# Two attention stages of a fused transformer kernel: fp32 products split in three rounded passes, PSUM banks shared out anew, work placed anew

## Chip, cores and metric

One core of one Trainium2 chip. The metric is the device time of one execution of the whole program in microseconds (median of several runs).

## Reference

The program computes two transformer layers on x of 4 x 2048 tokens of width 512. Each layer is cross attention (16 heads of width 32, 154 keys for each batch) on the layer-normed tokens, with a residual, then a feed-forward part: 32 experts with the top 8 of each token in layer 0, a light and a routed heavy branch in layer 1. The change touches the attention of both layers:

```python
q = split_heads(layernorm(x) @ Wq.T + bq)
k, v = split_heads(ctx @ Wk.T + bk), split_heads(ctx @ Wv.T + bv)
p = softmax((q @ k.T * tau + delta) / sqrt(32))
x = x + merge_heads(p @ v) @ Wo.T + bo
```

All is float32.

## The kernel before

`build` runs phases one after another: keys and values, `token_phase` of layer 0 (attention, and the logits of the gate), choice of the expert slots, the experts, `token_phase` of layer 1, the mixed phase (light branch) and the heavy phase. The change is in `token_phase` alone.

`token_phase` works on 16 groups of 512 tokens. Each engine runs one program of **turns** (i from -1 to 17), and a turn has 16 **units** (`st` or `u`): 4 heads (head group g = u // 4) of 128 tokens (t = u % 4). The order on each engine is written out by hand, by unit numbers; semaphores tie the engines together. In turn i, unit u:

- PE: `scores(i, u)`, four matmuls of 154 columns into two PSUM banks, 2*(u%2) and the next (so units alternate between banks 0, 1 and 2, 3); it waits for the exponentials of unit u-2. Then some of: `values` (P times V, five matmuls, lines 764 and 767), `x_turn` and `z_turn` (transposes, line 710), the gate's products. Then `streamed(st)`: half of one 512-column block of a dense product, which is k-chunks (0, 1) in an even unit and (2, 3) in an odd one. These are `query` (line 785, x @ Wq, for this group or the next) or `project` (line 806, O @ Wo, of the group before). Last `p_transposes` of unit u-2 (lines 734 and 735).
- DVE: `p_out` of unit u-3 (line 494: transposed P out of PSUM), `maximum` (line 471: the row maxima of the scores), `inverse` of unit u-1 (line 486), then what is placed there: layer-norm statistics (448), `normed` (460), `query_high` (69), `residual` (503), half of the transposed x out of PSUM (508), logits (521 to 532), in layer 1 `dot` (538).
- ACT: the four exponentials of a unit (line 691, each followed by a read of its accumulator), `query_out` (612), `o_out` (619: attention output out of PSUM), `p_tail_out` (624), the other half of the transposed x (629).
- POOL: `normalize` of unit u-1 (414: P times 1/sum), `query_low` (407), bias onto the residual (439), the powers of the norms (400).
- SP: all transfers in one queue. `stack_up(j, n)` (lines 339 to 349) lays head group n of q out as the stationary operand of the scores, 8 DMAs of the rounded part and 4 of the remainder; `load_kv`, the load of x, the load of x for the residual (`xbo`), and the stores of x and z.

The dense products take plain float32 operands. The profile shows each such matmul of 512 columns as two MATMUL records. In the experts and the heavy phase the same kind of product is already made by `product` (lines 72 to 76): each operand is split in a rounded part (`high`, type fp32r) and a remainder (`low`), and three passes are summed:

```python
pe.matmul(out, left[0], right[0], start=start, stop=False)
pe.matmul(out, left[0], right[1], start=False, stop=False)
return pe.matmul(out, left[1], right[0], start=False, stop=stop)
```

PSUM has 8 banks: 0 to 3 scores, 4 and 5 transposed P, 6 (`A_BANK`) dense products, 7 (`B_BANK`) the values' output and all other transposes, in turn.

Of the kernel before, what the change touches and what calls it, by code (L numbers as in the profile page):

```python
# [20 lines left out]
P = 128  # L21
# [9 lines left out]
TG = 4  # L31
# [213 lines left out]
def token_phase(nc, l, a, scr, c, x_in, x_rows):  # L245
    gate = l == 0
    with ExitStack() as ctx:
# [3 lines left out]
        wq, wo = sb("wq", [P, DC, D]), sb("wo", [P, DC, D])  # L251
# [4 lines left out]
        xn, xnT = sb("xn", [P, TG, D]), sb("xnT", [P, TG, D])  # L256
        oT = sb("oT", [P, 2, TG, D])
        qhigh, qlow = (sb(f"q_{part}", [P, 2, D], F32R) for part in ("high", "low"))
        qT = sb("qT", [P, 2, D])
        stack = sb("stack", [KROWS, HEADS, D], F32R)  # L260
# [13 lines left out]
        else:  # L274
# [5 lines left out]
                 "w_in wq_in kv_in0 kv_in1 kv_in2 kv_in3 x_in xbo_in ready ones x_stored z_stored "  # L280
                 "stacked0 stacked1 stacked2 stacked3 x_stats x_mv x_ve x_rstd xn xbo xnT_mm xnT_dve xnT_act "
                 "q_mm q_out q_high q_low scored negmax exped inv normed p_mm pTm pTt pv oT_out proj resid "
# [3 lines left out]
        W_IN = 16 * 4  # L286
        A_BANK, B_BANK = 6, 7
        STACK = 16 * 3 * HG
        Q_NEXT, Q_OWN = {10: 0, 14: 1}, {0: 2, 2: 3}
        O_AT, V_AT = {4: 0, 6: 1, 8: 2, 12: 3}, {7: 0, 11: 1}  # L290
        X_AT, Z_AT = {6: 0, 8: 1, 9: 2, 10: 3}, {2: 0, 4: 1, 5: 2, 12: 3}
# [18 lines left out]

        def load_kv(sp, j, g, used=0):
# [13 lines left out]
        def _(sp):  # L325
            sp.dma_start(x[:], rows(x_in, 0)).then_inc(s["x_in"], 16)
            sp.dma_start(wq[:], a[f"WqT{l}"].rearrange("(k p) n -> p k n", p=P)).then_inc(s["wq_in"], 16)
# [5 lines left out]
            sp.dma_start(wo[:], a[f"WoT{l}"].rearrange("(k p) n -> p k n", p=P)).then_inc(s["w_in"], 16)  # L333
# [5 lines left out]
            def stack_up(j, n):  # L339

                sp.wait_ge(s["q_high"], DC * j + n + 1)
                for at in (0, 2 * DK):
                    for h in range(HG):
                        sp.dma_start(stack[at:at + DK, HG * n + h, :].bitcast(F32),
                                     qhigh[h * DK:(h + 1) * DK, n % 2, :].bitcast(F32)).then_inc(s[f"stacked{n}"], 16)
                sp.wait_ge(s["q_low"], DC * j + n + 1)
                for h in range(HG):
                    sp.dma_start(stack[DK:2 * DK, HG * n + h, :].bitcast(F32),
                                 qlow[h * DK:(h + 1) * DK, n % 2, :].bitcast(F32)).then_inc(s[f"stacked{n}"], 16)

            def turn(i, par, prev2, prev, cur, nxt, nxt2):
                if cur:
                    stack_up(i, 1)
                if prev2 and gate:
                    sp.wait_ge(s["z"], TG * (i - 1))
                    sp.dma_start(rows(scr["xw"], i - 2, D), z[:]).then_inc(s["z_stored"], 16)
                if cur:
                    stack_up(i, 2)
                if prev and cur:
                    load_kv(sp, i, 2, GROUPS * i - 1)  # L360
                    load_kv(sp, i, 3, GROUPS * i)
                if nxt2:
                    reached(sp, s["xn"], TG * (i + 2))
                    sp.dma_start(x[:], rows(x_in, i + 2)).then_inc(s["x_in"], 16)
                if cur:
                    stack_up(i, 3)
                if cur and nxt:
                    load_kv(sp, i + 1, 0, GROUPS * i + 1)
                    load_kv(sp, i + 1, 1, GROUPS * i + 2)
                if nxt:  # L370
                    stack_up(i + 1, 0)
                if prev2 and not gate:
                    sp.wait_ge(s["z"], TG * (i - 1))
                    sp.wait_ge(s["score"], i - 1)
                    sp.dma_start(rows(scr["xs"], i - 2), z[:]).then_inc(s["z_stored"], 16)
                if prev:
                    sp.wait_ge(s["resid"], TG * i)
                    sp.dma_start(rows(x_rows, i - 1), xs[:]).then_inc(s["x_stored"], 16)
                if cur:
                    reached(sp, s["resid"], TG * i)  # L380
                    sp.dma_start(xbo[:], rows(x_in, i)).then_inc(s["xbo_in"], 16)

            turns(sp, turn)
# [4 lines left out]
        def _(pool):  # L388
# [14 lines left out]

            def query_low(j, n):
# [12 lines left out]
            def turn(i, par, prev2, prev, cur, nxt, nxt2):  # L417
                if isinstance(i, int) and i == 0:
                    pool.wait_ge(s["w_in"], W_IN)
                for st in range(UNITS):  # L420
                    if st == 3 and nxt:
                        rstd_of(0, "x", i + 1)
                    if st == 15 and prev:
                        rstd_of(1, "s", i - 1)
                    if st == 11 and prev2 and not gate:
                        pool.wait_ge(s["ssq_c"], i - 1)
                        pool.tensor_tensor(rn[:], ssq[:], half[:], ALU.pow).then_inc(s["rn"], 1)
                    if nxt and st == 12:
                        query_low(i + 1, 0)
                    if st >= 1 and cur:  # L430
                        normalize(i, st - 1)
                    if st == 0 and prev:
                        normalize(i - 1, UNITS - 1)
                    if cur and st in (0, 2, 4):
                        query_low(i, 1 + st // 2)
                    if st in (1, 5, 7, 9) and prev:
                        t = {1: 0, 5: 1, 7: 2, 9: 3}[st]
                        pool.wait_ge(s["xbo_in"], 16 * i)
                        pool.tensor_tensor(xbo[:, t, :], xbo[:, t, :], bo[:], ALU.add).then_inc(s["xbo"], 1)  # L439
# [4 lines left out]
        def _(dve):  # L444
# [23 lines left out]
            def maximum(i, u):  # L468
                dve.wait_ge(s["scored"], UNITS * i + u + 1)
                q = 2 * (u % 2)  # L470
                dve.tensor_reduce(negmax[:, u, :].rearrange("p (b h) -> p b h", b=2),  # L471
# [1693 lines left out]
```

## Time and profile before

| | |
|---|---|
| median of 3 runs | 3937.42 us (3932.35 to 3938.48) |
| the profiled execution | 3931.68 us, span 3930.0 us |
| mean granted TensorE clock | 0.947 of full speed |
| busy share: PE, DVE, POOL, ACT | 90%, 70%, 49%, 38% |
| token phase of layer 0 | about 120 to 1125 us |
| token phase of layer 1 | about 2202 to 3155 us |

A matmul's duration in the records is longer than its share of the engine, since matmuls overlap; what one costs is read from the starts of the records that follow one another. "x4" in a timeline is four records merged.

### The profile page before, as it was taken

Reading aid. Unit: us, or ns where it says so; the run is one execution under the profiler, and the core shown is the slowest. Engines: PE = TensorE matmul, PEld = TensorE weight load, DVE = VectorE, ACT = ScalarE, POOL = GpSimd, SP = SyncE. Lnnn points to the kernel's source line nnn. Section 1 sums busy time; section 2 is a strip of 40 time slices with the busy share of each in tenths; the row PEclk is TensorE's granted clock in tenths of the full one; section 3 lists DMA queues with packets and bytes.
Section 4 is the critical chain, followed back from the end, with each engine's and each line's share of the span. In section 5 each row is a group of like instructions: output and inputs, shape, how many; then the busy total and the mean of one; then the engine's idle time right before and its main releaser. Section 6 shows DMA issues by size and latency. Waiting matters only on the chain. (4 is left out here: it accounts for less than half of the span.)

```text
span 3930.0 us, 55737 instructions
## 1 busy us (share of the span) xinstructions
PE 3518.3 (90%) x16111; PEld 2376.0 (60%) x16111; DVE 2744.7 (70%) x5462; ACT 1506.5 (38%) x5254; POOL 1921.5 (49%) x1789
## 2 busy tenths in 40 slices
PE   8599999999946799999999599999999958879998
PEld 4355555555525677777777355555555536657776
DVE  3477777777669676776767367777777758766665
ACT  0256666666610111111111166666666634211110
POOL 0255555555510567677776355555565633223322
PEclk9799999999975899999999799999999979989999
DMA  5454555555420566666666444654654447521101
GB/s 162 134 146 139 144 161 141 144 156 146 119 76 11 156 162 163 161 165 169 155 173 149 109 133 134 172 146 133 169 153 141 131 147 273 188 97 22 18 12 14
DMA packets 323310, 523.14 MB, mean 133 GB/s; under 512 B 59352, under 2 KB 104216, under 8 KB 322648
## 3 DMA queue, kind: packets, MB, share of 16 engines
q1 hardware_dynamic: 290904, 443.79, 37.9%
q0 software_dynamic: 32256, 77.65, 10.4%
q8 instruction: 58, 0.95, 0.1%
q14 instruction: 92, 0.75, 0.1%
HBM read 283.64 MB, written 136.96 MB: 107 GB/s over the span
## 5 line engine op out<-in xcount | busy, mean ns | idle before, releaser
L691 ACT ACTIVATE t_pr<-ps,t_negmax 128x154 f32<-128x154 f32 x2048 | 867.8, 547 | 530.8 <-DVE t_negmax L471 530.4
L414 POOL TENSOR_TENSOR t_pr<-t_pr,t_inv 128x616 f32<-128x616 f32 x512 | 639.8, 1251 | 620.7 <-DVE t_inv L486 618.1
L494 DVE COPY t_pTm<-ps 128x512 f32<-128x512 f32 x512 | 350.0, 684 | 316.7 <-PE ps L735 312.6
L785 PE MATMUL ps<-t_xnT,t_wq 128*128 128x512 f32 x1024 | 506.2, 618 | 19.4 <-ACT t_qT L612 19.1
L806 PE MATMUL ps<-t_wo,t_oT 128*128 128x512 f32 x1024 | 501.1, 613 | 7.6 <-DVE t_xs L503 6.5
L734 PEld LDWEIGHTS ps<-ident,t_pr 128*128 128x128 f32 x2048 | 318.2, 204 | 295.6 <-issue 262.5
L691 ACT ACTIVATION_READ_ACCUMULATOR t_pr<-ps,t_negmax 128x1 f32 x2048 | 471.8, 230 | 0.0
L471 DVE TENSOR_REDUCE t_negmax<-ps 128x4 f32<-128x616 f32 x512 | 403.1, 787 | 28.5 <-PE ps L722 28.0
L734 PE MATMUL ps<-ident,t_pr 128*128 128x128 f32 x2048 | 334.2, 286 | 51.2 <-DVE t_pTm L494 37.6
L722 PE MATMUL ps<-t_kst,t_stack 98*128 98x154 f32 x2048 | 340.0, 289 | 13.4 <-DMA t_stack<-t_q_low 13.0
L785 PEld LDWEIGHTS ps<-t_xnT,t_wq 128*128 128x128 f32 x1024 | 176.9, 192 | 230.1 <-issue 203.4
L74 PE MATMUL ps<-e_xT_high,e_wgu_high 128*128 128x512 f32 x768 | 307.2, 400 | 1.6 <-DVE e_xT_low L1248 1.6
L76 PE MATMUL ps<-e_xT_high,e_wgu_low 128*128 128x512 f32 x768 | 304.7, 397 | 0.0
L75 PE MATMUL ps<-e_xT_low,e_wgu_high 128*128 128x512 f32 x768 | 302.7, 394 | 0.0
L806 PEld LDWEIGHTS ps<-t_wo,t_oT 128*128 128x128 f32 x1024 | 176.9, 192 | 186.8 <-issue 167.5
L722 PEld LDWEIGHTS ps<-t_kst,t_stack 98*128 98x128 f32 x2048 | 272.7, 194 | 19.2 <-issue 18.0
L1208 POOL DMA_INDIRECT x_dram<-e_y,e_put_idx x128 | 246.1, 1923 | 30.8 <-issue 30.5
L1316 ACT ACTIVATE e_sig<-ps 128x512 f32<-128x512 f32 x96 | 57.5, 599 | 527.4 <-PE ps L76 387.8
L407 POOL TENSOR_TENSOR t_q_low<-t_qT,t_q_high 128x512 fp32r<-128x512 f32 x128 | 176.3, 1377 | 167.5 <-DVE t_q_high L69 167.5
L1288 DVE TENSOR_TENSOR e_h<-e_sig,ps 128x512 f32<-128x512 f32 x96 | 65.8, 685 | 245.0 <-issue 200.4
L1937 POOL TENSOR_TENSOR h_w_low<-c_hw,h_w_high 128x512 fp32r<-128x512 f32 x64 | 89.6, 1403 | 249.0 <-DVE h_w_high L69 249.0
L439 POOL TENSOR_TENSOR t_xbo<-t_xbo,t_bo 128x512 f32<-128x512 f32 x128 | 166.2, 1300 | 62.4 <-DMA t_xbo<-x_dram 61.8
(297 smaller groups left out, 7297.0 us busy)
## 6 DMA issues: line engine op xcount, KB each, us to landing
t_stack<-t_q_high SPq DMA_DIRECT2D x1024, 64.0 KB, 2.1
e_wgu_in<-in_gate_upT SPq DMA_DIRECT2D x32, 1536.0 KB, 6.6
t_stack<-t_q_low SPq DMA_DIRECT2D x512, 64.0 KB, 2.0
x_dram<-t_xs SPq DMA_DIRECT2D x32, 1024.0 KB, 5.6
t_kst<-kst_dram SPq DMA_DIRECT2D x128, 235.8 KB
e_wd_in<-in_downT SPq DMA_DIRECT2D x32, 768.0 KB
xs_dram<-t_z SPq DMA_DIRECT2D x16, 1032.0 KB
l_z<-xs_dram SPq DMA_DIRECT2D x16, 1032.0 KB
```

The source lines that it names most:

```text
L74: pe.matmul(out, left[0], right[0], start=start, stop=False)
L75: pe.matmul(out, left[0], right[1], start=False, stop=False)
L76: return pe.matmul(out, left[1], right[0], start=False, stop=stop)
L414: pool.tensor_tensor(p, p, inv[:, v, :].unsqueeze(1).to_broadcast([P, KEYS, HG]), ALU.mult).then_inc(s["normed"], 1)
L471: dve.tensor_reduce(negmax[:, u, :].rearrange("p (b h) -> p b h", b=2), ps[:, q:q + 2, 0:2 * KEYS].rearrange("p b (h n) -> p b h n", h=2), ...
L494: dve.tensor_copy(pTm[:, g % 2, :, t * P:(t + 1) * P], ps[:, 4, :].rearrange("p (h n) -> p h n", h=HG)).then_inc(s["pTm"], 1)
L691: op = act.activation(pr[:, u % 4, :, h], ps[:, 2 * (u % 2) + h // 2, at:at + KEYS], ACT.Exp, bias=negmax[:, u, h:h + 1], accum_out=total[ ...
L722: mm = pe.matmul(ps[:, 2 * (u % 2) + h // 2, at:at + KEYS], stack[:, HG * g + h, t * P:(t + 1) * P], kst[:, g, h * KEYS:(h + 1) * KEYS], s ...
L734: pe.transpose(ps[:, 4, h * P:(h + 1) * P], pr[:, v % 4, 0:P, h], ident[:])
L785: mm = pe.matmul(ps[:, A_BANK, :], wq[:, k, n * P:(n + 1) * P], xnT[:, k, :], start=(k == 0), stop=(k == DC - 1))
L806: mm = pe.matmul(ps[:, A_BANK, :], oT[:, par, k, t * P:(t + 1) * P], wo[:, k, :], start=(k == 0), stop=(k == DC - 1))
L1208: pool.indirect_dma_start(out=scr["x1"][:, :], out_offset=bass.IndirectOffsetOnAxis(ap=put_idx[:, n:n + 1], axis=0), in_=y[q][:, n, :], in ...
```

## The change

In both token phases:

- **Split products.** Wq and Wo lie in SBUF as `high` and `low` (fp32r). They are loaded into `xs` and `z` (free at the start) and split there: `weight_high` on ACT, `weight_low` on POOL, four chunks each. The transposed x is rounded out of PSUM by ACT (`x_turned`, all four chunks) and its remainder is made by DVE (`x_low`, four); attention output likewise (`o_out` on ACT, `o_low` on DVE, new, four in a turn). `query` and `project` call `product`: three passes for one float32 matmul. The copies of x's halves on DVE (line 508) go.
- **Scores on three banks.** Heads lie 170 columns apart in one flat range: a unit has three heads in a bank of its own and one in bank 1, which both units share. The matmul into bank 1 comes last and waits (`shared`) for the first exponential of the unit before, which reads that unit's head in bank 1.
- **Bank 3 for transposes** of x, z and the gate; `values` keeps bank 7.
- **x is normed in place** (`xn` goes), so the next load of x waits for the transposes; `stack` holds two head groups in place of four; `oT` holds six chunks.
- **New placement.** Jobs are placed by half unit (`at`, 0 to 31; what belongs to a unit on DVE, ACT and POOL runs at the odd half), in a table for each layer; the SP order is written out for each layer.

```diff
-        wq, wo = sb("wq", [P, DC, D]), sb("wo", [P, DC, D])
+        wq = [sb(f"wq_{part}", [P, DC, D], F32R) for part in ("high", "low")]
+        wo = [sb(f"wo_{part}", [P, DC, D], F32R) for part in ("high", "low")]
-        stack = sb("stack", [KROWS, HEADS, D], F32R)
+        stack = sb("stack", [KROWS, 2 * HG, D], F32R)
...
+        T_BANK, A_BANK, B_BANK = 3, 6, 7
+        APART, BASE, SHARED = 170, (2, 854), (3, 0)
         Q_NEXT, Q_OWN = {10: 0, 14: 1}, {0: 2, 2: 3}
+        O_AT = {4: 0, 6: 1, 8: 2, 12: 3}
+        V = (14, 23, 2, 7) if gate else (15, 23, 3, 7)
+        X = (12, 15, 18, 20) if gate else (12, 16, 18, 20)
+        Z = (3, 8, 10, 25)
+        OL = (19, 30, 4, 9) if gate else (18, 29, 6, 10)
+        RES = (12, 15, 20, 28) if gate else (12, 15, 20, 27)
+        XL = (14, 18, 19, 22) if gate else (15, 18, 19, 21)
+        QH = (23, 1, 8, 15) if gate else (23, 2, 7, 15)
+        LOG = 31
+        SX = (1, 2, 3, 5) if gate else (0, 1, 1, 3)
+        NX = (8, 8, 8, 8) if gate else (6, 7, 8, 8)
+        SS = (14, 23, 25, 29) if gate else (16, 20, 26, 31)
+        NZ = (0, 0, 1, 2) if gate else (3, 6, 6, 11)
+        QO = (22, 0, 1, 5) if gate else (21, 0, 2, 5)
+        QL = (25, 1, 9, 16) if gate else (26, 3, 9, 19)
+        XB = (7, 10, 11, 20) if gate else (0, 4, 14, 18)
...
             def second_layer(i, par, prev2, prev, cur, nxt, nxt2):
...
+                if cur and nxt:
+                    load_kv(sp, i + 1, 0, GROUPS * i + 1)
+                    load_kv(sp, i + 1, 1, GROUPS * i + 2)
+                if nxt2:
+                    load_x(i + 2)
+                if nxt:
+                    stack_up(i + 1, 0)
...
+            def x_low(j, k):
+                dve.wait_ge(s["xnT_high"], DC * j + k + 1)
+                dve.tensor_tensor(xnT[1][:, k, :], ps[:, T_BANK, :], xnT[0][:, k, :].bitcast(F32),
+                                  ALU.subtract).then_inc(s["xnT_low"], 1)
...
                 reached(pe, s["exped"], UNITS * i + u - 1)
-                for h in range(HG):
-                    at = (h % 2) * KEYS
-                    mm = pe.matmul(ps[:, 2 * (u % 2) + h // 2, at:at + KEYS], stack[:, HG * g + h, t * P:(t + 1) * P],
+                for n in range(HG):
+                    h = (n + 1 + SHARED[u % 2]) % HG
+                    at = BASE[u % 2] + h * APART
+                    if n == HG - 1:
+                        reached(pe, s["shared"], UNITS * i + u)
+                    mm = pe.matmul(flat[:, at:at + KEYS], stack[:, HG * (g % 2) + h, t * P:(t + 1) * P],
                                    kst[:, g, h * KEYS:(h + 1) * KEYS], start=True, stop=True)
...
-                    mm = pe.matmul(ps[:, A_BANK, :], wq[:, k, n * P:(n + 1) * P], xnT[:, k, :],
-                                   start=(k == 0), stop=(k == DC - 1))
+                    mm = product(pe, ps[:, A_BANK, :], [w[:, k, n * P:(n + 1) * P] for w in wq],
+                                 [v[:, k, :] for v in xnT], k == 0, k == DC - 1)
```

`V`, `X`, `Z` are the half units at which PE runs `values`, `x_turn` and `z_turn`; `OL`, `XL`, `RES`, `QH`, `SX`/`SS`, `NX`/`NZ` and `LOG` those at which DVE runs `o_low`, `x_low`, `residual`, `query_high`, the statistics, `normed` of x and z, and the logits; `QO` is `query_out` on ACT, `QL` and `XB` are `query_low` and the bias on POOL.

## Rows read from the trace of the kernel before

**Rows 1.** Busy time by window (PE, PEld, DVE, ACT, POOL): a stretch of each layer

```profile
2500.00:2620.00 120.00, 115.30 (x549) 67.28 (x548) 91.96 (x198) 81.10 (x321) 71.14 (x61) 0.99 0.53 147
...
500.00:620.00 120.00, 118.19 (x594) 70.42 (x593) 90.02 (x190) 72.36 (x292) 66.24 (x58) 1.00 0.52 150
```

**Rows 2.** Timeline of PE (start, us, op): same place of two turns, each layer

```profile
508.84 1.98 PE L785 MATMUL ps<-t_xnT,t_wq 128*128 128x512 f32 x4
...
510.66 0.63 PE L734 MATMUL ps<-ident,t_pr 128*128 128x128 f32 x4
...
568.16 1.98 PE L785 MATMUL ps<-t_xnT,t_wq 128*128 128x512 f32 x4
...
2507.29 1.99 PE L785 MATMUL ps<-t_xnT,t_wq 128*128 128x512 f32 x4
...
2564.38 1.98 PE L785 MATMUL ps<-t_xnT,t_wq 128*128 128x512 f32 x4
```

**Rows 3.** Group of lines of DVE, experts (busy, mean ns, idle before)

```profile
L1248 DVE TENSOR_TENSOR e_xT_low<-ps,e_xT_high 128x512 fp32r<-128x512 f32 x128 | 88.5, 691 | 4.4
```

**Rows 4.** Timeline of PE, one unit of layer 0

```profile
549.18 0.65 PE L722 MATMUL ps<-t_kst,t_stack 98*128 98x154 f32 x4
...
549.66 0.61 PE L710 MATMUL ps<-ident,t_z 128*128 128x128 f32 x4
...
550.11 1.88 PE L806 MATMUL ps<-t_wo,t_oT 128*128 128x512 f32 x4
...
551.83 0.63 PE L734 MATMUL ps<-ident,t_pr 128*128 128x128 f32 x4
...
552.33 0.65 PE L722 MATMUL ps<-t_kst,t_stack 98*128 98x154 f32 x4
```

**Rows 5.** Timeline of PE, expert phase, two matmuls six apart

```profile
1402.23 0.48 PE L74 MATMUL ps<-e_xT_high,e_wgu_high 128*128 128x512 f32 x1
...
1403.72 0.39 PE L74 MATMUL ps<-e_xT_high,e_wgu_high 128*128 128x512 f32 x1
```

**Rows 6.** PE groups, idle before: layer 0 500.5:619.2, then layer 1 2500:2620

```profile
L785 PE MATMUL ps<-t_xnT,t_wq 128*128 128x512 f32 x65 | 31.8, 610 | 1.2 <-ACT t_qT L612 1.2
...
L734 PE MATMUL ps<-ident,t_pr 128*128 128x128 f32 x128 | 20.4, 282 | 0.4 <-DVE t_pTm L494 0.2
...
L734 PE MATMUL ps<-ident,t_pr 128*128 128x128 f32 x132 | 21.2, 284 | 3.1 <-DVE t_pTm L494 3.1
```

**Rows 7.** Timelines of DVE and ACT, the same unit of layer 0

```profile
549.46 0.69 DVE L494 COPY t_pTm<-ps 128x512 f32<-128x512 f32 x1 [3.23 <-PE ps L735]
...
550.07 0.79 DVE L471 TENSOR_REDUCE t_negmax<-ps 128x4 f32<-128x616 f32 x1
...
550.89 0.54 ACT L691 ACTIVATE t_pr<-ps,t_negmax 128x154 f32<-128x154 f32 x1
```

**Rows 8.** Timelines of DVE, POOL and PE, layer 0; its start-up; its gate logits

```profile
521.41 3.77 DVE L460 TENSOR_SCALAR t_xn<-t_x,t_mv,t_rstd 128x512 f32<-128x512 f32 x4
...
522.53 1.46 POOL L407 TENSOR_TENSOR t_q_low<-t_qT,t_q_high 128x512 fp32r<-128x512 f32 x1
...
525.93 0.72 PE L734 MATMUL ps<-ident,t_pr 128*128 128x128 f32 x4 [0.22 <-DVE t_pTm L494]
...
133.33 1.91 DVE L460 TENSOR_SCALAR t_xn<-t_x,t_mv,t_rstd 128x512 f32<-128x512 f32 x4 [1.52 <-POOL t_rstd L400]
...
561.06 0.66 DVE L521 TENSOR_REDUCE t_logit<-ps 128x128 f32<-128x512 f32 x1
...
562.52 0.68 DVE L494 COPY t_pTm<-ps 128x512 f32<-128x512 f32 x1
```

**Rows 9.** Timelines of SP and PE, layer 1, the end of a turn

```profile
2568.80 4.96 SPq L344 DMA_DIRECT2D t_stack<-t_q_high  x8
...
2573.80 2.49 SPq L348 DMA_DIRECT2D t_stack<-t_q_low  x4
...
2577.98 0.65 PE L722 MATMUL ps<-t_kst,t_stack 98*128 98x154 f32 x4
```

More of the change, by code:

```diff
@@ L352, in turn @@
                 if cur:
                     stack_up(i, 1)
-                if prev2 and gate:
-                    sp.wait_ge(s["z"], TG * (i - 1))
-                    sp.dma_start(rows(scr["xw"], i - 2, D), z[:]).then_inc(s["z_stored"], 16)
+                    stack_up(i, 2)
+                if prev and cur:
+                    load_kv(sp, i, 2, GROUPS * i - 1)
+                if cur:
+                    stack_up(i, 3)
+                if prev2:
+                    store_z(i - 2, i - 1)
@@ L357, in turn, with second_layer @@
+            def second_layer(i, par, prev2, prev, cur, nxt, nxt2):
+                if cur:
+                    stack_up(i, 1)
+                if prev and cur:
+                    load_kv(sp, i, 2, GROUPS * i - 1)
                 if cur:
@@ L369, in turn @@
                     load_kv(sp, i + 1, 1, GROUPS * i + 2)
+                if nxt2:
+                    load_x(i + 2)
                 if nxt:
                     stack_up(i + 1, 0)
[L372 to L375, printed above, removed]
+                if prev2:
+                    store_z(i - 2, i - 1)
+                if cur:
+                    load_xbo(i)
                 if prev:
[L377 to L383, printed above, removed]
+                    store_x(i - 1)
+            turns(sp, first_layer if gate else second_layer)
             sp.wait_ge(s["z_stored"], 16 * NG)
@@ L417, in turn @@
             def turn(i, par, prev2, prev, cur, nxt, nxt2):
+                if isinstance(i, int) and i == -1:
+                    for k in range(DC):
+                        pool.wait_ge(s["wq_high"], k + 1)
+                        weight_low(wq, xs, k, "wq_low")
                 if isinstance(i, int) and i == 0:
@@ L430, in turn @@
[L430 to L439, printed above, removed]
+                    if isinstance(i, int) and i == 0 and 6 <= st < 6 + DC:
+                        pool.wait_ge(s["wo_high"], DC)
+                        weight_low(wo, z, st - 6, "wo_low")
@@ L579, in turn @@
-                    if prev and st in (6, 8, 10, 14):
-                        t = min(st - 6, 6) // 2
+                        for t in range(TG):
+                            if at == SX[t]:
+                                statistics(0, "x", i + 1, x, (t,))
+                        for t in range(TG):
+                            if at == NX[t]:
+                                normed(0, "x", i + 1, x, x, "xn", (t,))
+                    if at in SS and prev:
+                        t = SS.index(at)
@@ L805, in project, with x_turn @@
                 for k in chunks:
[L806 to L807 removed]
+                    mm = product(pe, ps[:, A_BANK, :], [v[:, o_slot(par, k), t * P:(t + 1) * P] for v in oT],
+                                 [w[:, k, :] for w in wo], k == 0, k == DC - 1)
                 if DC - 1 in chunks:
                     mm.then_inc(s["proj"], 1)
[L811 removed]
+            def x_turn(j, k, prev2):
```

406 lines of the change are left out of this document (218 added, 188 removed).

## Prediction

> **What bounds the kernel now.** I read the busy time by window first. In a stretch of 120 us of the token phases PE is busy for 118.2 us in layer 0 and 115.3 us in layer 1, DVE for 90.0 and 92.0, POOL for 66 and 71 [rows 1]. So PE sets the pace of both phases, and DVE is next with a quarter of its time free. Then the timeline of PE: the same matmul comes back after 568.16 - 508.84 = 59.32 us in layer 0 and after 57.09 us in layer 1 [rows 2]; that is one turn, and there are 16 in each layer. PE's own waits are about 0.95 us a turn in layer 0 (its groups' idle times in two turns sum to 1.9; the largest is 1.2 for `query_out`) and about 2.3 us in layer 1 (4.8 in 2.1 turns; 3.1 of it in the transposes of P, for DVE's copy) [rows 6].
>
> **The products.** A chunk of a dense product (two float32 matmuls, four records) takes 551.83 - 550.11 = 1.72 us behind transposes [rows 4], and 510.66 - 508.84 = 1.82 us behind other matmuls [rows 2]. The three-pass form of the same size runs in the experts: six passes behind transposes take 1403.72 - 1402.23 = 1.49 us [rows 5]. So a chunk gets shorter by 0.23 to 0.33 us; I take 0.29, nearer the second, since most chunks stand behind scores or values. A layer has 16 x 16 chunks, two layers 512: **-148 us** (bounds -118 and -169).
> The Trainium skill (TensorE: Matmul & The Clock Gate, "Back-to-back issue gap") gives N/2.4 + 2.5 ns for one pass, 216 ns here; six would be 1.30 us and the saving at 0.42 to 0.52 us a chunk some 240 us, an estimate from that page. The row shows 1.49 us with the weight loads in it, and the sum goes by the row.
>
> **The work that is added.** DVE loses two copies a turn and gains four `x_low` and four `o_low`: an instruction of that kind takes 691 ns [rows 3], and one such step 0.61 us from start to start (550.07 - 549.46) [rows 7], so some +4 us a turn. DVE had 90.0/120 x 59.32 = 44.5 us in a turn [rows 1, 2]; it will have 48.6 of the 54 to 55 that PE then takes in layer 0, and about 48 (92.0/120 x 57.09 = 43.8, and 4) of 52 in layer 1. ACT gains two copies on 36 us of busy time a turn, POOL nothing in a steady turn: both stay hidden behind PE. DVE no longer is: at 90% what counts is when each job comes.
>
> **How late DVE may be.** In a plain unit PE will take 0.48 (scores, 549.66 - 549.18) + 1.46 (a chunk, between 1.40 and 1.49) + 0.50 (transposes of P, 552.33 - 551.83) = 2.45 us [rows 4]. DVE's fixed part is `p_out` 0.61, `maximum` 0.70, `inverse` 0.09: 1.40 us. The new wait `shared` ties the last score matmul of unit u+1 to the maximum and first exponential of unit u. Counted from the scores' start at 549.18: maximum over and ACT at it at +1.71 [rows 7], the first exponential with its read over at about +2.3; PE gets there at 2.45 + 0.37 = +2.8. So **DVE may be late by 0.5 us** and what PE has between (transposes 0.44, values 1.98). Before, PE waited for the unit before that, and only `p_out` bound it: a norm of four tiles that held DVE for 3.7 us cost PE 0.22 us [rows 8].
>
> **Layer 0, unit by unit** (DVE's jobs by the placement against PE's time; 0.6 us for a statistics, residual or low job, 0.4 for `query_high`). Into unit 0 come the logits, 1.46 us [rows 8], and two norms of z. One tile of `normed` takes 1.91/4 = 0.48 us where POOL is idle and 3.77/4 = 0.94 where POOL works beside it [rows 8]. The norms behind the logits come when POOL's `normalize` is over, so they cost 0.48 each: 1.4 + 1.46 + 1.0 = 3.9 us against PE's 2.9. The 1.0 us of lateness goes into 0.5 of slack and into PE's wait for `query_out`, which was 0.6 and stays. Unit 1: two statistics, two norms, `query_high`, 4.7 us against 2.45, late by 2.8; PE has values and transposes there (2.4 + 0.5), so no stall, with nothing to spare. Unit 2 wins it back. Unit 4: four norms (3.7) and `query_high`, 5.5 us against 4.4, after 1.0 us of lateness from unit 3, with a slack of 0.94: a stall of 1.1. The rest fits. Sum 1.7 us; with the norms at 0.94 throughout it is 3.5. I take **2.4 us a turn** where it was 0.95.
> The Trainium skill (SBUF — State Buffer, "Who interferes with whom") has it that a copy or scalar operation of VectorE in a two-port mode and an instruction of GpSimd exclude each other, and that the one issued second waits for the whole of the first. The trace agrees, with 3.77 us against 1.91 for the same four norms; if it holds at each place, the stall of a turn is nearer 1.7 than 3.5 us.
>
> **Layer 1.** Unit 4 (three of the norms of x) is late by 1.3 to 1.9 us with a slack of 0.5: 0.8 to 1.4. And the stack: `stack_up` of group 0 for the next turn took SP 4.96 + 2.49 us, its last DMA was issued at about 2575.7 and PE began the next turn's scores at 2577.98, just behind its landing: no slack [rows 9]. Now its place is behind `load_kv`, which waits for the values at half unit 23, now behind the chunk, and behind the load of x. From unit 11's scores: values over 3.9, `load_kv` 1.65, `load_x` 0.6, stack 7.5, landing of the last 1.4: +15.1; PE is there after 4.4 + 4 x 2.45 = 14.2. So 0.9 us for it, which takes the place of the wait for `query_out`. **2.4 us a turn** where it was 2.3.
>
> **Once a layer.** Four `weight_low` on POOL (1.4 us each, as [rows 8]) stand before the first `rstd`, 5.5 us, of which half is hidden by the loads and by the shorter fill of `stack`; each first transpose of x now waits for ACT and DVE in turn. 3 to 8 us, taken as 5: **+10 us** in all.
>
> **Sum.** -148 + 16 x (2.4 - 0.95) + 16 x (2.4 - 2.3) + 10 = -148 + 23 + 2 + 10 = -113 us on the profiled 3931.7: 3819. The median of the runs shown lies 5.7 us above that execution, so the time forecast is **3824 us**, 2.9% less. The layer-0 turn would be 59.3 - 4.6 + 1.4 = 56.1 us, the layer-1 turn 57.1 - 4.6 + 0.1 = 52.6 us.
>
> **Rivals.**
> *A: the placement is exact and PE waits for almost nothing.* For it: every large DVE job stands where PE has values or transposes beside it, and ACT's waits for a query stand likewise. Against it: my sums for unit 4 in both layers. All waits but 0.6 us a turn go: -148 - 52 + 19 + 10 = -171, 3766 us.
> *B: DVE is the bound, at 90% in order.* Norms and copies run into POOL, each late unit stalls PE by `shared` instead of being won back. Layer 0 at 4.5 us of waits, layer 1 at 4.5: -148 + 57 + 35 + 10 = -46, 3891 us. For it: a slack of 0.5 us where it was over 1.5. Against it: the free units 5 to 9 and 12 to 15.
> *C, slower than before: the queue of SP becomes the pace.* With two groups in `stack` a group can be laid out only when the group two before is scored, and each takes 7.5 us of SP's issue, on top of `query_low` on POOL and the landing, with `load_kv` and whole loads of x between. My sums leave 2 to 4 us in every group but the one above. It decides where each group is late by 1.5 us: 6 us a turn more in 32 turns is +192 on 3824 less the 29 counted, 3987; the point of no gain is 3.5 us a turn beyond my sum. Against it: SP is issuing for some 39 of 55 us (four groups of 7.5, twelve loads of keys and values at 0.55, four large transfers at 0.6).
> *D: the change does not do what it says*, and the passes here cost no less than float32. The scores are of that type already and the experts run it; what could eat the gain is the added wait inside each unit: nothing, or at most half of a score matmul (0.48/4/2 = 0.06 us) x 512 = 30 us. That is in the range.
>
> **Numbers.** About 0.2% (8 us) is what a measurement of this kernel can tell from no change. Chances: the forecast (3790 to 3860) 0.50, A 0.20, B 0.20, C 0.08, D 0.02. Faster by over 0.2%: 0.88; within: 0.03; slower: 0.09. The range that should hold 8 in 10 reaches from A to B: 3765 to 3890 us.
>
> **What would show it.** In the changed profile the starts of product passes should lie 0.23 to 0.25 us apart, in sixes of 1.40 to 1.49 us. The turns should be 56 and 52.6 us. DVE's share in a turn should be 87 to 92%. The score group of line 722's successor should show idle time ended by ACT's exponential (`shared`) at units 1 to 5, and in layer 1 a wait for a stack DMA at the start of a turn. Idle time of over 4 us a turn on PE would prove me wrong towards B, with SP's rows ending it towards C; under 1 us, towards A.

## The result and the profile after

The changed kernel takes 3956.7 us (median of 4 runs, 3950.9 to 3961.4) where the kernel before takes 3934.9 (4 runs beside them): ratio 1.0057, 95% interval 1.004 to 1.0073. The forecast was 3824 us and 88% for faster. It is slower by 0.6%, with an interval that leaves out 1, and the time lies 67 us above the range of 3765 to 3890.

The page of the changed kernel, its first two parts:

```profile
span 3949.2 us, 58011 instructions
...
PE 3417.9 (87%) x17135; PEld 2612.1 (66%) x17135; DVE 2848.8 (72%) x5654; ACT 1543.9 (39%) x5334; POOL 1930.6 (49%) x1805
...
PEclk9799999999975799999999799999999979989999
```

The same two stretches as in [rows 1], busy time by window (PE, PEld, DVE, ACT, POOL, then the granted clock, the DMA share and GB/s):

```profile
500.00:620.00 120.00, 108.52 (x633) 81.75 (x631) 90.53 (x191) 70.40 (x284) 63.00 (x56) 0.94 0.51 142
2500.00:2620.00 120.00, 108.60 (x626) 82.50 (x625) 102.26 (x210) 84.19 (x328) 70.16 (x61) 0.97 0.53 151
```

PE was busy for 118.2 and 115.3 us of the 120; now it is for 108.5 and 108.6, and its granted clock is 0.94 and 0.97 where it was 1.00 and 0.99. So PE stands still for some 11 us in each stretch. The waits of the two token phases tell for what (us in total, times, longest), first layer 0 (320 to 1100 us), then layer 1 (2350 to 3140 us):

```profile
PE ps L847 <- DVE t_pTm L583: 33.6, 17, 5.9
DVE t_z L549 <- issue: 33.1, 5, 6.7
...
PE ps L835 <- DMA t_vt<-vt_dram: 26.4, 13, 4.4
...
PE ps L74 <- ACT t_qT L713: 6.6, 13, 0.5
```

```profile
POOL t_xbo L528 <- DMA t_xbo<-x_dram: 96.8, 14, 7.9
...
PE ps L847 <- POOL t_pr L494: 50.1, 14, 4.6
...
PE ps L74 <- ACT t_qT L713: 8.1, 13, 1.0
PE ps L835 <- ACT t_pr L778: 6.9, 13, 0.5
```

Three waits stand out, and none of them has a term in the forecast's sum.

**Stall 1, every second turn of layer 0.** The turns of layer 0 (from a `values` matmul to the same one a turn later) take 56 and 66 us in alternation. The loop over turns holds two of them, and the long one is where it jumps back. DVE and PE there:

```profile
503.71 0.17 DVE L627 COPY c_top<-t_top 128x32 f32 x1
510.49 1.00 DVE L549 TENSOR_SCALAR t_z<-t_xs,t_mv,t_rstd 128x512 f32<-128x512 f32 x2 [6.60 <-issue]
```

```profile
512.14 1.13 PE L847 MATMUL ps<-ident,t_pr 128*128 128x128 f32 x4 [5.83 <-DVE t_pTm L583]
...
514.05 2.00 PE L857 MATMUL ps<-t_pTt,t_vt 104*128 104x512 f32 x2
...
552.22 1.02 PE L857 MATMUL ps<-t_pTt,t_vt 104*128 104x512 f32 x2
```

The last instruction of the body ends at 503.88, the first of the next pass starts at 510.49, and the profile finds no semaphore for it ("issue"). PE stands still for 5.83 us and then works at half speed: the same `values` matmuls take 2.00 us at 514 and 1.02 at 552. The window after the stall shows a granted clock of 0.50 for 6 us, the level of 1.2 GHz (the kernel before has 1.00, the level of 2.4 GHz, at the same place of its turn, 510 to 516 us):

```profile
512.00:518.00 6.00, 5.86 (x20) 2.68 (x20) 5.92 (x12) 1.72 (x9) 3.29 (x3) 0.50 0.27 66
```

So the long turn is 10 us longer for 6.6 us on DVE. At the same jump the kernel before lost 0.33 us (its timeline of DVE):

```profile
503.11 0.17 DVE L532 COPY c_top<-t_top 128x32 f32 x1
503.61 0.69 DVE L494 COPY t_pTm<-ps 128x512 f32<-128x512 f32 x1 [0.33 <-issue]
```

Two things stand beside the stall of the changed kernel. SP had just issued three transfers of 1 MB (store of x, load of x, load for the residual); and among the packets of 502 to 512 us there are four of the kind "instruction", of which the kernel before has none there:

```profile
497.49 0.43 SPq L402 DMA_DIRECT2D x_dram<-t_xs  x1
498.19 0.41 SPq L398 DMA_DIRECT2D t_x<-in_x  x1
498.79 1.17 SPq L406 DMA_DIRECT2D t_xbo<-in_x  x1
```

```profile
q14 instruction: 4, 0.03, 1.0%
```

**Stall 2, every turn of layer 0.** PE at unit 12, and SP's queue just before:

```profile
554.75 0.27 PE L848 MATMUL ps<-ident,t_pr 128*104 128x128 f32 x1
557.28 0.68 PE L835 MATMUL ps<-t_kst,t_stack 98*128 98x154 f32 x4 [2.25 <-DMA t_vt<-vt_dram]
```

```profile
550.26 0.43 SPq L391 DMA_DIRECT2D xw_dram<-t_z  x1
550.88 0.34 SPq L359 DMA_DIRECT2D t_kst<-kst_dram  x1
551.41 0.76 SPq L359 DMA_DIRECT2D t_vm<-vm_dram  x1
552.35 1.06 SPq L359 DMA_DIRECT2D t_vt<-vt_dram  x1
```

The keys and values of head group 3 are loaded behind the store of 1 MB of z, and PE reaches them 2.25 us before they have landed.

**Stall 3, every turn of layer 1.** POOL, PE and SP at the start of a turn:

```profile
2594.38 1.26 POOL L528 TENSOR_TENSOR t_xbo<-t_xbo,t_bo 128x512 f32<-128x512 f32 x1 [7.19 <-DMA t_xbo<-x_dram]
2595.60 2.38 POOL L494 TENSOR_TENSOR t_pr<-t_pr,t_inv 128x616 f32<-128x616 f32 x2
```

```profile
2596.87 0.91 PE L847 MATMUL ps<-ident,t_pr 128*128 128x128 f32 x4 [3.82 <-POOL t_pr L494]
```

```profile
2585.08 0.44 SPq L394 DMA_DIRECT2D xs_dram<-t_z  x1
2585.72 0.39 SPq L406 DMA_DIRECT2D t_xbo<-x_dram  x1
```

The first bias of layer 1 stands at half unit 0 (`XB = (0, ...)`). Its load is issued at 2585.72, behind another store of 1 MB, and lands at about 2594. POOL stands in that wait for 7.19 us, and `normalize` of two units stands behind it on POOL (the "x2" at 2595.60): PE waits 3.82 us for P.

What was forecast of the passes is there too. Six passes of a chunk (layer 0, at another place of the same turn) take 552.22 - 550.78 = 1.44 us; behind the first, their starts lie 0.23 us apart (four of the six shown):

```profile
550.78 0.44 PE L74 MATMUL ps<-t_xnT_high,t_wq_high 128*128 128x512 f32 x1
551.06 0.39 PE L75 MATMUL ps<-t_xnT_low,t_wq_high 128*128 128x512 f32 x1
551.29 0.39 PE L76 MATMUL ps<-t_xnT_high,t_wq_low 128*128 128x512 f32 x1
551.52 0.39 PE L74 MATMUL ps<-t_xnT_high,t_wq_high 128*128 128x512 f32 x1
```

### The profile page after: what moved, and what is told of

Its sections match the earlier page's. It is cut to its first block and busy times, and to the rows that moved or that the text cites. A ratio compares the mean times of both kernels' runs of the same rounds, so it can differ in the third digit from the quotient of the medians.

```text
span 3949.2 us, 58011 instructions
## 1 busy us (share of the span) xinstructions
PE 3417.9 (87%) x17135; PEld 2612.1 (66%) x17135; DVE 2848.8 (72%) x5654; ACT 1543.9 (39%) x5334; POOL 1930.6 (49%) x1805
## 5 line engine op out<-in xcount | busy, mean ns | idle before, releaser
L778 ACT ACTIVATION_READ_ACCUMULATOR t_pr<-ps,t_negmax 128x1 f32 x2048 | 484.7, 237 | 0.0
L847 PE MATMUL ps<-ident,t_pr 128*128 128x128 f32 x2048 | 357.7, 299 | 111.4 <-POOL t_pr L494 57.2
L835 PE MATMUL ps<-t_kst,t_stack 98*128 98x154 f32 x2048 | 365.3, 298 | 59.9 <-DMA t_vt<-vt_dram 28.0
L835 PEld LDWEIGHTS ps<-t_kst,t_stack 98*128 98x128 f32 x2048 | 291.3, 201 | 76.8 <-DMA t_vt<-vt_dram 31.5
L1400 ACT ACTIVATE e_sig<-ps 128x512 f32<-128x512 f32 x96 | 57.5, 599 | 527.2 <-PE ps L76 527.2
L74 PE MATMUL ps<-t_xnT_high,t_wq_high 128*128 128x512 f32 x512 | 228.1, 446 | 18.6 <-ACT t_qT L713 18.6
L74 PE MATMUL ps<-t_wo_high,t_oT_high 128*128 128x512 f32 x512 | 221.6, 433 | 4.7 <-DVE t_xs L592 4.7
L75 PE MATMUL ps<-t_xnT_low,t_wq_high 128*128 128x512 f32 x512 | 210.1, 410 | 0.0
L76 PE MATMUL ps<-t_xnT_high,t_wq_low 128*128 128x512 f32 x512 | 209.9, 410 | 0.0
L76 PE MATMUL ps<-t_wo_high,t_oT_low 128*128 128x512 f32 x512 | 206.3, 403 | 0.0
```

Of the source, the lines that this page charges most:

```text
L778: op = act.activation(pr[:, u % 4, :, h], flat[:, col:col + KEYS], ACT.Exp, bias=negmax[:, u, h:h + 1], accum_out=total[:, u, h:h + 1])
L835: mm = pe.matmul(flat[:, at:at + KEYS], stack[:, HG * (g % 2) + h, t * P:(t + 1) * P], kst[:, g, h * KEYS:(h + 1) * KEYS], start=True, sto ...
L847: pe.transpose(ps[:, 4, h * P:(h + 1) * P], pr[:, v % 4, 0:P, h], ident[:])
```

## Experiments

Each time stands against runs of the kernel before on the same chip (3931 to 3934 us).

### One repair at a time, and all three

```diff
# e1: VectorE's turns written out
-            turns(dve, turn)
+            unrolled(turn)
# e2: first_layer, layer 0
+                if prev and cur:
+                    load_kv(sp, i, 3, GROUPS * i)
                 if prev2:
                     store_z(i - 2, i - 1)
-                if prev and cur:
-                    load_kv(sp, i, 3, GROUPS * i)
# e3: the bias of layer 1 later
-        XB = (7, 10, 11, 20) if gate else (0, 4, 14, 18)
+        XB = (7, 10, 11, 20) if gate else (7, 10, 14, 18)
# e4: e1, e2 and e3
```

> The changed kernel with DVE's program of the token phases written out turn by turn (as ACT's is) in place of a hardware loop over two turns; the instructions of a turn and their order are the same. Theory J (in layer 0 DVE stands still for some 6.6 us at the top of every second turn because after the jump back its instructions have to be fetched, behind 3 MB of data transfers just issued): layer 0's turns stop alternating between 56 and 66 us, all are about 56, the idle time before the norm of z ended by nothing that the profile shows is gone, and the time falls by 45 to 60 us. Rival Z (DVE waits there for the store of the z before, or for the transposes of z): the stall stays, the time moves by less than 8 us.

> The changed kernel with, in layer 0's queue of SP, the load of keys and values of head group 3 issued before the store of z, not behind it. Theory K (the 2.0 us a turn for which PE waits at unit 12 for that load are due to the 1 MB store issued just before it): that wait is gone, the time falls by 20 to 30 us. Rival (the values' end releases the buffer too late, or PE then waits for DVE at the same place): the wait shrinks by less than 1 us or is given back, the time falls by less than 10 us.

> The changed kernel with the first two additions of the bias onto the residual on POOL, layer 1, at half units 7 and 10 in place of 0 and 4 (as in layer 0), so POOL no longer stands waiting for the load of the residual before it normalizes P. Theory X (that wait, 7 us a turn on POOL, makes PE wait 3.6 to 3.8 us a turn in its transposes of P): PE's wait for POOL there is gone, layer 1's turns fall from 57.3 to 53 to 54 us, the time by 45 to 60 us. Rival B (DVE, full to 88%, is the bound of the turn whoever waits): PE waits for DVE's copies or maxima at that place, layer 1's turns fall by less than 1.5 us, the time by less than 20 us.

> The three edits together. If the three waits are independent, as the theories have it, their gains add: some 115 to 140 us less than the changed kernel, near 3825 us, which is 2.5 to 3% faster than the kernel before and what the prediction had summed. If DVE is the bound behind them (rival B), it stays above 3890 us.

`e4` is all of these edits in one kernel. The turns are read from the `values` matmuls of the profiled executions.

| kernel | median, us | ratio to before, 95% | turns of layer 0 | turns of layer 1 |
|---|---|---|---|---|
| changed | 3956.7 | 1.0057 (1.004 to 1.0073) | 56 / 66 | 57.0 to 57.5 |
| e1 | 3912.2 | 0.9941 (0.9924 to 0.9957) | 55.8 to 58.7 | 57.3 to 58.4 |
| e2 | 3917.9 | 0.9964 (0.995 to 0.9978) | 55.0 / 62 to 64 | 57.2 to 57.6 |
| e3 | 3888.3 | 0.9876 (0.9858 to 0.9894) | 56 / 66 | 52.7 to 52.8 |
| e4 | 3815.4 | 0.9694 (0.9677 to 0.971) | 54.9 to 56.3 | 52.7 to 53.5 |

Each stall goes with its own repair, and the steady turns of the other layer stay what they were. Alone the repairs are worth 44, 39 and 68 us (expected were 45 to 60, 20 to 30 and 45 to 60), together 141, 3956.7 - 3815.4, which is 10 us less than the sum of the three. In layer 1, e3 takes the turn to 52.7 us, where 52.6 was forecast; in layer 0, e4 takes it to about 55.5, where 56.1 was forecast. The three stalls are the whole distance between the forecast (3824 us) and the result; what lies under that agreement is taken up further down.

### What makes stall 1: the transfers, the jump, or the place of the code

```diff
# e5: layer 0, in the looped turns; e9: the same for load_x too
-                sp.dma_start(xbo[:], rows(x_in, j)).then_inc(s["xbo_in"], 16)
+                if gate and not isinstance(j, int):
+                    sp.dma_start(xbo[:, :, 0:P], rows(x_in, j, P)).then_inc(s["xbo_in"], 16)
```

> The changed kernel, but the residual's load of layer 0 brings only a quarter of its columns in the looped turns, so three quarters of the residual of layer 0 are left out (later results are then not the reference's). It asks why DVE stands still for 6.6 us at the start of every second turn of layer 0. Theory 1 (its instructions are fetched after the jump of its loop, behind three transfers of 1 MB that SP issued just before): with 2.25 MB instead of 3 in front of it the stall gets shorter, to about 4 us or less, the turns of 66 us become 62 to 64, and the time falls by 15 to 30 us from 3957. Theory 2 (the jump costs what it costs, whatever is being moved): the stall stays at 6 to 7 us, the turns at 66 us, the time within 5 us of 3957.

> The changed kernel, but in the looped turns of layer 0 both loads of x (for the norm and for the residual) bring a quarter of their columns, so three quarters of both are left out there. Bringing a quarter of the residual's load alone changed nothing, although the queues were empty some 3 us earlier; in the changed kernel four instruction packets lie at the jump of VectorE's loop (505.4, 506.9, 508.0, 510.9 us, the jump at 503.8), in the kernel before none. Theory 1 (the jump makes VectorE fetch its code anew, and the two loads of 1 MB in front stretch each fetch): with 0.5 MB in front the stall of 6.6 us falls to 3 us or less, the turns of 66 us to 62 or less, the time by 20 to 35 us from 3957. Theory 2 (the fetches follow each other at their own latency): the stall stays at 6 to 7 us and the time within 5 us of 3957.

Both kernels leave out three quarters of the columns of the loads named, so their output is not the reference's.

e5: 3958.0 us, ratio to before 1.0065 (1.005 to 1.0081): nothing gained, DVE's five waits sum to 32.9 us where they were 33.1. That is theory 2. e9: 3951.0 us, ratio 1.0047 (1.003 to 1.0064); the five waits sum to 26.1 us, the long turns are 64 us, the four instruction packets are still there. This lies between the two expectations. The jump at 498 us:

```profile
497.84 0.17 DVE L633 COPY c_top<-t_top 128x32 f32 x1
502.69 1.00 DVE L555 TENSOR_SCALAR t_z<-t_xs,t_mv,t_rstd 128x512 f32<-128x512 f32 x2 [4.68 <-issue]
```

The DMA engines are all but idle from 499.3 us on, but 4.7 of the 6.6 us are left. So the transfers stretch the stall by up to 2 us, and do not make it.

```diff
# e7: the kernel before
-            turns(dve, turn)
+            unrolled(turn)
# e10: the changed kernel, ahead of the turns
+            if gate:
+                for _ in range(64):
+                    dve.wait_ge(s["x_in"], 16)
             turns(dve, turn)
# e11: the kernel before, in DVE's turn
+                    if gate and prev2 and st in (3, 6, 9, 12):
+                        dve.wait_ge(s["x_in"], 16)
```

> The kernel before, with VectorE's turns written out instead of looped, the same edit that gave the changed kernel 44 us. Theory 1 (the stall comes of the changed order of SP's queue, three large transfers in front of the jump): the kernel before lost 0.33 us there in a turn pair of layer 0, and 1.4 us in seven places of layer 1, so nothing or at most 10 us is gained, 3921 to 3935 us. Rival (unrolled code is better for VectorE whatever the queue does): 30 us or more are gained here too, 3900 us or less.

> The changed kernel with 64 waits that are long fulfilled ahead of VectorE's turns of layer 0: they move its loop by 64 instructions and do nothing else, for at most 2 us once. Theory 3 (whether the jump finds its target still held depends on where the loop's code lies): the four instruction packets at each jump and the stall of 6.6 us go in layer 0, 30 to 45 us are gained, 3912 to 3927. Rival (the place has no part in it, only the length of the body, 293 instructions where it was 286, or what SP moves at the time): the stall stays, 3952 to 3960.

> The kernel before with four waits that are long fulfilled in each of VectorE's turns of layer 0, so that its loop's body has 294 instructions, as the changed kernel's (293), where it has 286. Theory 4 (the body became too long to be held over the jump): stalls and instruction packets appear at each jump of layer 0, 3 to 7 us each, and the time rises by 15 to 40 us from 3934. Rival (the length has no part in it): no stall over 1 us at the jump, and the time within 5 us of 3934.

e7: 3933.5 us, ratio 1.0 (0.999 to 1.0009). Written-out turns are worth nothing by themselves; e1's gain is the stall.

e10: 3926.7 us, ratio 0.9984 (0.9972 to 0.9995), 30 us less than the changed kernel. It has the same body and the same transfers, and some waits more ahead of the loop. The same jump, and the instruction packets around it:

```profile
497.84 0.17 DVE L627 COPY c_top<-t_top 128x32 f32 x1
498.50 1.00 DVE L549 TENSOR_SCALAR t_z<-t_xs,t_mv,t_rstd 128x512 f32<-128x512 f32 x2 [0.48 <-issue]
```

```profile
q14 instruction: 1, 0.01, 0.2%
```

In layer 0 the stall is down to 0.48 us, with the three transfers in full in front of it. And a new one has come in layer 1, whose code was moved along with the rest; its sum is 17.5 us in five places:

```profile
2447.89 0.69 DVE L537 BATCH_NORM_STATS2 t_stat<-t_x 128x6 f32<-128x512 f32 x1 [3.69 <-issue]
```

e11: 3969.5 us, ratio 1.0091 (1.0074 to 1.0108), 36 us more than the kernel before, for waits that are long fulfilled and of which no other effect is seen. The jump of layer 0 there:

```profile
509.95 0.17 DVE L532 COPY c_top<-t_top 128x32 f32 x1
517.02 0.69 DVE L494 COPY t_pTm<-ps 128x512 f32<-128x512 f32 x1 [6.91 <-issue]
```

```profile
517.77 1.13 PE L736 MATMUL ps<-ident,t_pr 128*128 128x128 f32 x4 [4.92 <-DVE t_pTm L494]
```

Its turns are 59.2 and 67 us in alternation, as those of the changed kernel are 56 and 66. So stall 1 has nothing to do with products, banks or the placement on PE.

What the long jumps have in common can be read from the records. The trace has the loop's branch itself and the first register operation of the body behind it. The nine looped runs have 90 such jumps in the two token phases. In 50 of them 0.22 to 0.29 us pass between the two, with no instruction packet in that time; in 40 of them 3.5 to 6.8 us pass, with one to three packets of 8 KB in it. Over four passes of the loop of layer 0 (380 to 860 us) there are 11 instruction packets in the kernel before, 32 in the changed one, 12 in e10 and 31 in e11; in layer 1 (2450 to 2920 us) there are 12, 12, 33 and 15. So a pass with a long jump brings some five packets, 40 KB, that one with a short jump does not bring. That VectorE fetches its code anew, since the target is no longer held, fits all of this. It remains an inference, since the records do not say for which engine a packet was.

Length and place both matter. The waits of e11 stand only in turns that have a group two before them, and the first of these is in the loop: the recorded instructions ahead of the loop are those of the kernel before, and its body has 290 where it was 286 (294 had been expected). So e11 changes the length alone, and the stall comes. e10 changes the place alone, by 32 recorded instructions, and the stall goes in layer 0 and comes in layer 1. The length by itself does not decide either: the body in layer 1 of the changed kernel has 298 and no stall, that in layer 0 has 293, in the changed kernel with the stall and in e10 without it. By what rule length and place go together no run here tells.

### Is PE's work the bound?

```diff
# e6: one pass, both products; project alike
-                    mm = product(pe, ps[:, A_BANK, :], [w[:, k, n * P:(n + 1) * P] for w in wq],
-                                 [v[:, k, :] for v in xnT], k == 0, k == DC - 1)
+                    mm = pe.matmul(ps[:, A_BANK, :], wq[0][:, k, n * P:(n + 1) * P], xnT[0][:, k, :],
+                                   start=(k == 0), stop=(k == DC - 1))
```

> The changed kernel with one pass instead of three in the products of q and o, so the two passes with a remainder are left out and q and the attention output carry the rounding of one operand pair. It asks what would bound the token phases if PE had 4 of 6 passes less in each chunk, 0.93 us. If PE's own work set all of the time, 512 chunks would give up to 475 us. Theory 1 (DVE, at about 48 of 56 us a turn, takes over almost at once): turns of layer 1 stay above 50 us, those of layer 0 too, and the whole gain is under 150 us. Theory 2 (PE's work is the bound and the late loads only add to it): turns of 45 us or less and a gain of over 300 us.

The kernel leaves out the two passes with a remainder. 3892.8 us, ratio 0.9895 (0.988 to 0.991): 64 us less than the changed kernel, for 512 x 0.93 = 476 us of work on PE less at the full clock. Turns are 55 to 57 and 62 to 63 us in layer 0 and 55 to 57 in layer 1, as theory 1 had it. Two things take the rest back. PE now waits for DVE (61.7 us for the copy of P in layer 1, where the changed kernel has 4.8), for `stack` (18.3 us there, 3.0 in the changed kernel) and for keys and values (51.1 us in layer 0, 26.4 in the changed kernel). And PE's granted clock is lower: 0.86 in the stretch of layer 0 and 0.84 in that of layer 1, where the changed kernel has 0.94 and 0.97. In 120 us of layer 1 some 31 us of passes are left out (14.9 us a turn), and PE is busy for only 12.7 us less (95.9 against 108.6). So the run shows that taking work from PE gives little while the stalls stand. How much of that is DVE and how much the clock it does not separate, and theory 1's reason, that DVE takes over, is shown in part only.

### A version better than both, and the products undone in it

```diff
# e8: e4, and first_layer loads x ahead of the first stack of the next turn
+                if nxt2:
+                    load_x(i + 2)
                 if nxt:
                     stack_up(i + 1, 0)
                 if prev:
                     store_x(i - 1)
-                if nxt2:
-                    load_x(i + 2)
# e12: e8, each chunk a float32 matmul of the rounded parts; project alike
+                    mm = pe.matmul(ps[:, A_BANK, :], wq[0][:, k, n * P:(n + 1) * P].bitcast(F32),
+                                   xnT[0][:, k, :].bitcast(F32), start=(k == 0), stop=(k == DC - 1))
```

> The changed kernel with all three repairs (VectorE's turns written out, the third load of keys and values ahead of the store of z in layer 0, the bias of layer 1 at half units 7 and up), and in layer 0 the load of x also ahead of the first stack of the next turn, some 8 us earlier. With the three alone DVE still waited 27.1 us in 12 places for x, and PE's waits for the copy of P and for the norm of z behind it came to 15 and 14 us in 13 turns. Theory 1 (x comes late and makes the units 2 to 4 late): DVE's wait goes and 8 to 20 us are gained on 3815, so 3795 to 3807. Rival (DVE wins the lateness back, PE has its work): within 5 us of 3815.

> The kernel with the three repairs and the earlier load of x (3798.6 us), with one part of the change undone: each chunk of q and o is again a plain float32 matmul (four records of 128 rows' width in place of six passes), on the rounded operands alone, so what the remainders add is left out; VectorE and ScalarE make the remainders all the same. It measures the one large term of the prediction by itself, 0.29 us a chunk in 512 chunks, -148 us (bounds -118 and -169). Theory (PE's work sets the pace once the stalls are gone): the time rises by 118 to 169 us, 3917 to 3968, the turns of layer 0 from 54.0 to 58 to 59 us, those of layer 1 from 52.7 to 57 us. Rival (VectorE, at over 90% in layer 1, had become the bound, and the passes' gain is partly lost to it): the rise is under 100 us.

e8: 3798.6 us, ratio 0.9655 (0.964 to 0.967), 17 us less than e4, as theory 1 said. The turns of layer 0 are 54.0 us throughout, DVE's wait for x is gone. The two stretches of before and after in e8:

```profile
500.00:620.00 120.00, 118.05 (x723) 90.19 (x722) 102.54 (x218) 81.42 (x330) 74.17 (x64) 1.00 0.56 153
2500.00:2620.00 120.00, 114.35 (x674) 85.88 (x666) 111.59 (x227) 92.04 (x361) 79.57 (x67) 1.00 0.57 159
```

e12: 3890.7 us, ratio 0.989 (0.9873 to 0.9906). It leaves out what the remainders add. Without the passes 92 us come back (104 between the two profiled executions). That is below the 118 to 169 of the theory and on the side of the rival (under 100 us: the gain is partly lost to VectorE). Where they are was read from the starts of PE's matmuls: time from the first of a group to the start of the next other group, us a turn, mean of 8 turns from 400 us and 8 from 2400 us on. A wait ahead of a group is counted with the group before it.

```
                        before      e12 float32    e8 passes
layer 0   turn          59.3        57.7           54.0
          products      28.8        28.1           24.2
          scores         9.2         8.5            8.9
          P transposed   8.1         8.2            8.6
          x, z transp.   3.7         3.6            3.2
          values         8.0         7.9            7.9
layer 1   turn          58.0        55.2           52.8
          products      31.1        28.2           24.6
          scores         8.6         8.7            9.8
          P transposed   8.2         8.7            9.1
```

From e12 to e8 the products give 4.0 and 3.6 us a turn, 0.25 and 0.22 a chunk. The transposes of x and z give another 0.4 and 0.3, since the passes start sooner behind them. The scores (with them the wait `shared`, and in layer 1 the stack) take back 0.4 and 1.1, the transposes of P 0.4 in each. From before to e12, with the products as they were, 42 us are gained, some 17 of them by the earlier load of x that e12 has from e8. In the steady turns that is 1.6 us in layer 0 and 2.8 in layer 1; over all 16 turns of a layer (first to last `values`) 16 and 33 us, of which the profiled execution of e12 gives 15 back outside the turns. The rest is the sum of the new placement, the banks and x normed in place, which were not taken apart.

## Why the prediction was wrong

**What came out, and how much of it by luck.** PE is the bound of layer 0 once the stalls are gone (118.05 us of 120 in e8), and the passes take what was read for them. The sum, 3824 us, is near e4 with 3815, and the two turns are near too: 52.7 us in layer 1 of e3 for 52.6, and about 55.5 in layer 0 of e4 for 56.1. The agreement is better than the working behind it, in three places.

- The turn of layer 1 before was read as 57.09 us from one pair of matmuls, and that was a short one. From 2507.29 us on the same matmul starts at 2564.38, 2623.37, 2680.88 and 2739.84 us, so turns of some 57 and 59 us alternate, with a mean of 58.1. The turn fell by 5.3 us, where 4.5 was forecast.
- In layer 0 PE waits about 2 us a turn in e4, where 2.4 was taken, but for another reason. The forecast had late norms stall PE at `shared`. In the steady turns of e4 (430 to 960 us) PE waits 10.3 us for the copy of P, 5.0 for `query_out`, 3.2 for the norm of z, and never for an exponential. A large part is a load again: DVE waits 27.1 us in 12 places for x, and with x loaded earlier (e8) PE waits 3.6 us in ten turns for the copy of P, about 1 us a turn in all.
- In layer 1 (2400 to 2930 us of e4) PE waits about 2.3 us a turn, where 2.4 was taken. 0.5 of it is for the stack, where 0.9 was taken, and 0.6 for the exponential: there `shared` shows.

The rule of the Trainium skill (SBUF — State Buffer, "Who interferes with whom"), by which 1.7 us would have been nearer in layer 0, is not decided by this, since the waits left there are in good part those of the load of x.

**The steps that failed.**

1. *"ACT gains two copies [...], POOL nothing in a steady turn: both stay hidden behind PE."* POOL's work is the same, but its first bias was moved to half unit 0 and its load stands behind the store of z in SP's order, so a wait was put in front of two `normalize`. POOL waits 96.8 us for that load in 14 turns, PE waits 50.1 us for P behind it, and it is worth 68 us (e3). The kernel before had such a wait on POOL too, up to 6.2 us, but PE was hardly held up by it (3.0 us in all); why not was not looked into:

```profile
POOL t_xbo L439 <- DMA t_xbo<-x_dram: 53.8, 14, 6.2
...
PE ps L734 <- POOL t_pr L414: 3.0, 4, 0.9
```

2. *"Layer 0, unit by unit (DVE's jobs by the placement against PE's time)."* Only DVE's jobs were laid against PE. The loads of SP in layer 0 were not, though the order of its queue stood in the change: group 3 behind the store of z, 39 us (e2). In layer 1 the stack's transfers were laid against PE, and that term had the right place and half the size (0.5 us for 0.9).
3. The jump of VectorE's loop was put at nothing, without a word on it. It cost 44 us (e1), of a cause that has nothing to do with what the change is for (e10, e11). The trace of the kernel before shows 0.33 us there, and nothing in it could have given the 6.6 us.
4. The term of the products was mis-sized. Taken as -148 us (bounds -118 and -169), it measures -92 to -104 in e12 against e8. Over whole turns a chunk goes from 1.76 us (e12) to 1.51 and 1.54 us (e8), so it gives 0.22 to 0.25 us, near the lower bound of 0.23, and 0.8 and 1.5 us a turn come back as waits of the scores and of P. Against it the rest of the change gave -42 us in e12, -25 without the earlier load of x, where the other terms of the sum were +35. The two errors cancel in large part. That is luck, and e4 lies nearer to the forecast for it than either term was to its size. The estimate by the Trainium skill (TensorE: Matmul & The Clock Gate, "Back-to-back issue gap"), 0.42 to 0.52 us a chunk, is further off: its gap for an isolated matmul is 216 ns, and the starts of passes here lie 230 ns apart.
5. *Once a layer*, taken as +10 us: in e8 the start-up and all that lies outside the 16 turns is 3 us longer than before.

**The rivals.** C, slower through SP's queue, had 0.08. The sign is its own, and so is the queue for stalls 2 and 3 (transfers that stand too late in it), but not its mechanism: the stack was never the pace, and PE waits for it 3.0 us in all in layer 1. B (DVE the bound) is not it, with DVE at 75 to 85% of the stretches; after the repairs it is near, at 93% in layer 1 of e8. D (passes that cost no less) is refuted by the 92 us of e12. The range left out any late transfer outside the stack; the two that were late cost 39 and 68 us, enough to leave the range without the jump.

## What to carry to other kernels

When a change rewrites an order of transfers or a placement, lay each queue against its consumers, not only the engine that is next to be the bound: for every moved DMA, what is queued ahead of it, when it lands, and which in-order engine stands in the wait for it with other work behind. Here three small edits were worth 141 us, so compare a rewritten schedule with its late loads repaired before judging the idea in it.

Look at the back edge of an engine's hardware loop in the trace before and after any edit of that engine's code, even of one that adds only fulfilled waits; written-out turns cost nothing here (e7) and take the risk away.

## What the runs showed of the hardware

- A jump of VectorE's loop of 286 to 298 recorded instructions takes 0.22 to 0.29 us from its branch to the first instruction behind it, or 3.5 to 6.8 us with instruction packets in between. More length at the same place turned the one into the other (e11), and so did another place at the same length (e10). With less data in flight the stall was up to 2 us shorter (e9). TensorE's loop, with 1171 to 1416 recorded instructions in the kernel before and the changed one, weight loads included, shows no such stall in either.
- Behind a stall of PE of 5.8 us the granted clock is 0.50 for 6 us, and `values` matmuls take 2.00 us in place of 1.02; behind a stall of 3.8 us (layer 1) the next 6 us have 0.72:

```profile
2597.00:2603.00 6.00, 6.00 (x29) 5.33 (x30) 4.63 (x6) 2.78 (x10) 5.92 (x6) 0.72 0.30 71
```

- With less work on PE and the same stalls its clock went down, not up: 0.84 to 0.86 in the stretches of e6, 0.94 and 0.97 in the changed kernel, 1.00 in e8.
- Behind four float32 transposes a product starts 0.07 us sooner when its operands are fp32r than when they are float32: 0.37 us after the first transpose (500.37 us in e8) against 0.44 us (516.41 in e12). The transposes themselves take the same 0.61 us in both.
